# First aggregation of a two-layer graph network: transposes two turns later, dense steps on a longer and later schedule

## The reference, cut to what matters

```
h = layernorm(x)                          # 6250 x 256
agg = segment_sum(h[src], dst, 6250)      # gather 106250 rows, add them per target node
h = (1 + eps1) * h + agg
h = relu(h @ W1a + b1a)                   # 256 -> 512, first layer
h = relu(h @ W1b + b1b)                   # 512 -> 512, second layer
t = h @ W2a                               # 512 -> 512, third layer, gathered in the next stage
own = (1 + eps2) * t + b2a                # a node's own row for the next stage
```

## Time and profile before

| | us |
|---|---|
| median of 3 runs | 4498.23 (4498.11 to 4499.08) |
| span of the profiled execution | 4526.2 |
| first aggregation in it, start to end | about 76 to 1334 |
| second aggregation | about 1334 to 2620 |
| third aggregation | about 2780 to 4060 |

### The profile page before, as it was taken

One profiled execution on the slowest core, in us unless ns is written; L12 is line 12 of the kernel. 1 busy time (PEld: TensorE's weight loads), 2 busy tenths in 40 slices (PEclk: granted clock), 3 DMA queues, 4 the chain that ended last, 5 costly groups with the idle time before them and its releaser, 6 DMA issues. The chain is left out here.

```text
span 4526.2 us, 40559 instructions
## 1 busy us (share of the span) xinstructions
PE 3407.3 (75%) x12357; PEld 2256.3 (50%) x12359; DVE 1481.5 (33%) x5707; ACT 497.8 (11%) x1161; POOL 2794.2 (62%) x2815
## 2 busy tenths in 40 slices
PE   3577777878878889899999976566556656658997
PEld 2354444545453444444444455345444444438986
DVE  5112121212121433444333445234343343442221
ACT  4010000000110000000000002000000000003432
POOL 4666666666646666666666502666666666635664
PEclk7788888988889999999999987777777778769998
DMA  6333333433349666666666527334334333327887
GB/s 199 90 112 112 111 110 110 131 111 111 109 128 330 194 198 200 193 190 194 195 201 205 170 104 240 108 114 123 115 117 128 115 114 114 119 80 174 203 210 188
DMA packets 321341, 687.10 MB, mean 152 GB/s; under 512 B 58976, under 2 KB 148300, under 8 KB 320854
## 3 DMA queue, kind: packets, MB, share of 16 engines
q0 software_dynamic: 169712, 474.01, 37.9%
q10 hardware_dynamic: 86448, 110.35, 7.4%
q1 hardware_dynamic: 64970, 100.14, 6.8%
HBM read 592.43 MB, written 99.13 MB: 153 GB/s over the span
## 5 line engine op out<-in xcount | busy, mean ns | idle before, releaser
L280 POOL DMA_INDIRECT s_edge_rows<-table,w_src_idx x2538 | 2495.4, 983 | 1235.3 <-issue 712.6
L320 PE MATMUL s_psA<-s_edge_rows,s_onehot 128*128 128x257 f32 (+2 forms) x4932 | 1695.0, 487 | 212.1 <-DMA s_edge_rows<-table,w_src_idx 92.3
L320 PEld LDWEIGHTS s_psA<-s_edge_rows,s_onehot 128*128 128x128 f32 x4932 | 1012.6, 210 | 758.6 <-issue 635.1
L295 DVE TENSOR_SCALAR s_onehot<-w_iota_row,w_dst_l 128x128 f32<-128x128 bf16 x2466 | 531.6, 296 | 28.5 <-PEq L149 16.4
L2031 POOL DMA_INDIRECT acc_rows<-s_y,s_tnode x105 | 166.3, 1584 | 130.7 <-DVE s_y L2154 98.8
L1011 PE MATMUL s_psM<-s_h1T,s_w1b 128*128 128x512 f32 (+2 forms) x448 | 195.2, 582 | 52.5 <-ACT s_h1T L913 49.0
L330 PE MATMUL s_psA<-s_edge_rows,s_early 128*128 128x257 f32 (+2 forms) x648 | 221.3, 468 | 10.2 <-issue 9.0
L1017 PE MATMUL s_psM<-s_w2a,s_hT 128*128 128x512 f32 x392 | 196.3, 647 | 22.7 <-issue 16.6
L2179 PE MATMUL s_psU<-s_xT,s_w 128*128 128x128 f32 x1680 | 208.2, 278 | 0.2 <-ACT s_xT L2085 0.2
L2179 PEld LDWEIGHTS s_psU<-s_xT,s_w 128*128 128x128 f32 x1680 | 199.3, 195 | 0.6 <-issue 0.6
L2189 PE MATMUL s_psD<-moe_w,s_hT 128*128 x840 | 199.5, 381 | 0.0
(11 more groups left out here) (364 smaller groups left out, 2802.6 us busy)
## 6 DMA issues: line engine op xcount, KB each, us to landing
s_w<-in_L_ffn_W_dram SPq DMA_DIRECT2D x105, 512.0 KB
s_edge_rows<-table,w_src_idx POOLq DMA_INDIRECT x2538
s_swT<-swt_rows SPq DMA_DIRECT2D x12, 1024.0 KB
table<-s_trow ACTq DMA_DIRECT2D x11, 1024.0 KB
own_rows<-s_own ACTq DMA_DIRECT2D x11, 1024.0 KB
s_self_h<-own_rows ACTq DMA_DIRECT2D x11, 1024.0 KB
swt_rows<-s_swT ACTq DMA_DIRECT2D x11, 1024.0 KB
extra_rows<-w_zeros SPq DMA_DIRECT2D x7, 896.0 KB
```

What stands on the lines that cost most here:

```text
L280: pool.indirect_dma_start(self.rows[:, g % self.SLOTS, t, :], None, self.table, bass.IndirectOffsetOnAxis(ap=src_idx[:, at:at + 1], axis=0 ...
L295: last = nc.vector.tensor_scalar(into[:, t, :], iota_row[:, q * P:(q + 1) * P], dst_l[:, at + t:at + t + 1], None, ALU.is_equal)
L320: last = nc.tensor.matmul(banks[b % 2][:, 0:w], self.onehot[:, g % self.AHEAD, t, :], self.rows[:, g % self.SLOTS, t, col:col + w], start= ...
```

## The change

`pipeline` gets three arguments. `close_at` is the turn of the next block at which PE and ACT close a block: 3 instead of 1 in the first aggregation. `first` is the first turn on which steps fall: 4 instead of 2. `late` is a number of steps beyond `STEPS` that are taken one superblock later, together with the first steps of the next: 3. The three lists of steps are longer. The stores go from step 21 to step 24. DVE goes on closing a block at its first turn. The other two aggregations call `pipeline` as before.

```diff
-        def pipeline(group, close, piece, begin=None, close_first=False):
+        def pipeline(group, close, piece, begin=None, close_first=False, late=0, close_at=1, first=2):
+
+            def pieces(s, k):
+                if 0 <= s < len(SUPER):
+                    piece(s, k)
+                if 0 <= s - 1 < len(SUPER) and k < late:
+                    piece(s - 1, STEPS + k)
...
-                    if g == 1 and b and not close_first:
+                    if g == close_at and b and not close_first:
                         close(b - 1)
                     for k in range(STEPS):
-                        if s and i == 2 + k * (len(turns) - 2) // STEPS:
-                            piece(s - 1, k)
+                        if s and i == first + k * (len(turns) - first) // STEPS:
+                            pieces(s - 1, k)
             close(NB - 1)
             for k in range(STEPS):
-                piece(len(SUPER) - 1, k)
+                pieces(len(SUPER) - 1, k)
+            for k in range(late):
+                pieces(len(SUPER), k)
...
-            FIRST, SECOND, THIRD = (0, 1, 2, 3), (5, 7, 9, 11), (14, 16, 18, 20)
+            FIRST, SECOND, THIRD, STORED = (1, 2, 3, 4), (7, 9, 11, 13), (17, 19, 21, 23), 24
+            LATE_STEPS = STORED + 1 - STEPS
...
-                    if k == STEPS - 1:
+                    if k == STORED:
                         act.wait_ge(s_hi, b0 + nb)
...
-                pipeline(lambda b, g: None, close, piece)
+                pipeline(lambda b, g: None, close, piece, late=LATE_STEPS, close_at=3, first=4)
...
-                pipeline(group, close, piece, close_first=True)
+                pipeline(group, close, piece, close_first=True, late=LATE_STEPS, first=4)
...
-                pipeline(group, close, piece)
+                pipeline(group, close, piece, late=LATE_STEPS, close_at=3, first=4)
```

## The result

The changed kernel took 4510.72 us (median of 6, 4504.86 to 4513.52) against 4497.49 us of the kernel before (6, 4489.10 to 4499.08) on the same chip: ratio 1.0033, interval 1.0022 to 1.0044. By the ratio it is slower by 15 us (10 to 20), by the medians by 13, where 21 us less was forecast.

What follows compares the result with a forecast made beforehand. The prediction took POOL's gathers to pace the first aggregation, with ring waits costing about 138 us. 4526 less 22 for the ring plus 1 for the end gave 4505 profiled, 4477 for the runs; range 4428 to 4515 us.

Steps and rivals of the forecast that it cites:

- The 22 us of the ring: First aggregation: POOL's stalls for a free ring place, costing about 138 us, fall from 44 to 37, gaining 22 us.
- the 1 us of the end: After POOL's last gather in the first aggregation: PE's remaining work is the same in any order; 1 us charged for waits.
- nothing moves: Rival, first aggregation: PE's word gets through when POOL falls quiet, PE waits elsewhere; 4490 to 4507 us, chance 0.25.
- The sign written down for it: Sign of no change: PE's waits gone from line 990 and back at 1005 or 1011, POOL's waits still near 138.
- Transposes two turns later: PE before the transposes, line 990: waits for DVE's sum at most half of 80.1 us; first layer may take some over.
- Second layer a turn further off: PE before the second layer, line 1011: one more group, 1.3 us, off waits averaging 7.0 us; 49.0 us in 7.
- The bank `psM[3]`, the rival for slower: First layer's last quarter waits about 3 us in each of eleven superblocks for its bank; 4532 or 4515 us; slower's chance 0.20.
- A rule against the row: PE clock, first aggregation: fewer waits would raise it from 0.86 to 0.95, some 7 us per superblock; sum unchanged.
- The sum: Whole kernel: 4526 - 22 + 1 = 4505 us profiled; runs lie 28 us below, so 4477.

Runs made afterwards that it cites:

- the first experiment: Changed kernel with the old plan (transposes at turn 1, steps from turn 2) in the last three superblocks; 4082.59 against 4084.18 us for the kernel before, ratio 0.9999.

## Why the prediction went wrong

Two terms failed. The 22 us of the ring made the forecast a gain, and without them it would have been no change; the 1 us of the end hid the loss.

*"The end of the stage ... its remaining work is the same in any order ... I charge 1 us."* This is the step that hid the loss. The end grew by 6.4, 7.8 and 9.3 us on chips 1, 3 and 4. I looked at what lies behind POOL's last gather and took it as given; but how much lies there is set by what PE could do in the three short superblocks before it. PE is full there, so it can't catch up on what a turn without steps leaves undone. The charge of 1 us was for waits in a row where groups lay between, and these measured 1.3 (chip 1) and 1.95 us (chip 3). Put at nothing were PE's lateness at the last gather, 3.5 and 3.85 us, and the lower granted clock in the last layers, 1.6 and 1.3 us. The runs that exchange only the three short superblocks bear it out: without the new turns there 0.9999 and 1.0001, and with them alone 1.0018, against 1.0032 for the whole change on the same chip. The two intervals overlap, and the second aggregation starts at the same time in both.

*"What the ring gains ... 7 x 3.1 = 22 us."* This is the step that failed first. It measured nothing: from 138 to 141 us net on chip 1, from 134 to 137 on chip 4. The assumption that PE would have done one to two groups more when its word gets through was worked out from one stall, and no run bears it out: PE's waits moved and did not end earlier. The reading that POOL's waits are no echo of PE's waits was right, and it should have been followed to its end: if they are not, shortening PE's waits by 4 us each can't lengthen POOL's runs either. The rival "nothing moves" had this mechanism, and the evidence it named, three aggregations of equal length, was sound. The sign written down for it came true to the letter: waits gone from line 990 and back at 1005, POOL's waits near 138. Only its time, 4490 to 4507, missed the end.

*Transposes two turns later.* The local forecast held: at most half of 80.1 us was expected at line 990, and 1.9 were named there. The remark that the first layer may take over what the transposes no longer wait for came true, 30.5 to 94.6 us.

*Second layer a turn further off.* 49.0 us named fell to 8.9, and 52.2 in all to 23.4, as expected; worth nothing.

*The bank `psM[3]`, the rival for slower.* It is there, 8.4 us in 2 waits on chip 1 (8.1 in 5 on chip 4), and not at the size named. The late fourth block is in the kernel of the first experiment and costs nothing that can be measured. So this rival had the side right, and by luck: its mechanism is not the one that cost the time.

*A rule against the row.* The granted clock of the stage stayed at 0.86 on chip 1, where the changed kernel's waits of PE moved from one step to another. At the very end the clock did count, for the worse: 1.6 of the 6.4 us. No run here shows what fewer waits on such a chip would give.

*The sum.* 4477 was forecast, 4510.7 measured. Of the 34 us between them 22 are the gain that wasn't there and 5.4 the end beyond the 1 us charged. The other 6 are not located. On chip 3 too the medians differ by 11.4 us where the second aggregation starts 7.1 later; two sets of runs of the same kernel differed by 4.0 and 3.5 us there and on chip 4. The range, 4428 to 4515, took the result in only through the rivals that had another mechanism.

## What to carry to other kernels

A plan of turns that is stretched for a long steady part is stretched in its short last rounds too, and here it cost 6 to 9 us there: look at the rounds in which the engine that works alone at the end is already full, and leave those as they were. And a wait that goes away is worth only what the pacing engine's own waits show afterwards; here 98 us of PE waits left one line and 29 another, 64 came back at the first layer and 56 at the edge sums, with no effect on POOL. A stall seen on one chip should be checked on another before a schedule is built on it.

## What the runs showed of the hardware

The same kernel took 4497 and 4493 us on chips 1 and 4 and 4084 and 4085 us on chips 2 and 3. The difference lies in the three aggregations: POOL waits 134 to 141 us net for the ring in the first on chips 1 and 4 and not at all on 2 and 3, with the same 1.26 us from gather to gather. Each start of ACT's ReLU behind the first layer can be set against the modelled end of the product that it waits for, in the kernel before and up to the last gather. On chip 1, 27 of 48 start more than 1 us late, the mean of all is 4.6 us and the longest 19.2; on chip 4 it is 23 of 48 and 17.6. On chip 3 all of them start 0.04 us after it. After the last gather the delay is 0.04 us on chips 1 and 4 too. So on two of four chips the other engines act on PE's work late, and in this stage only while POOL's gathers run. Whether the products end later than their modelled ends or their signals travel late, the rows don't tell. The packets of the gathers' queue took as long on chip 1 as on chip 3 (159 to 163 ns on average, in the kernel before). What makes the chips differ stays open; nothing in these runs could separate it further. The effect of the change didn't depend on it: 1.0033, 1.0032 and 1.0038.

The granted clock was lower on chip 1 in each aggregation, and PE waited more there: 313 us in the first, against 197 on chip 3. It was 0.86, 0.95 and 0.76 in the three on chip 1, and on chip 3, for the kernel before:

```profile
62.00:1137.00 1075.00, 884.79 (x2913) 565.54 (x2914) 242.71 (x1077) 125.44 (x208) 816.18 (x847) 0.94 0.46 130
1170.00:2310.00 1140.00, 1096.66 (x3219) 572.23 (x3220) 500.87 (x1544) 94.13 (x151) 866.68 (x848) 0.98 0.75 230
2494.00:3574.00 1080.00, 695.09 (x2646) 511.66 (x2646) 471.42 (x2102) 37.98 (x106) 822.27 (x847) 0.89 0.47 138
```

The columns are the stretch and its length, then busy us and instructions of PE, PE's weight loads, DVE, ACT and POOL, then granted clock, DMA share and GB/s.
